# Splits of turned queries and outputs and the addition of normed sums, moved from VectorE to GpSimd

## The reference

```
cq = rms_norm(hidden_states @ w_qa.T, q_a_ln_w)
q = (cq @ w_qb.T).reshape(b, s, H, DQ).transpose(0, 2, 1, 3)
q_pe = q_pe * cos + rotate_half(q_pe) * sin
...
scores = jnp.einsum('bhqd,bhkd->bhqk', q_full, k_full) * scale
scores = jnp.where(causal, -jnp.inf, scores)
attn = jax.nn.softmax(scores.astype(jnp.float32), axis=-1)
out = jnp.einsum('bhqk,bhkd->bhqd', attn, v)
return out @ w_o.T
...
x = x + _layernorm(_L0_attn_ref(_layernorm(x, axis=-1), ...), axis=-1)
```

## Time and profile before

| | us |
|---|---|
| median of 3 runs | 1697.91 |
| lowest to highest | 1697.68 to 1703.39 |
| the profiled execution, its own time | 1701.13 |
| its span on the core | 1699.4 |
| VectorE busy, whole span | 1182.0 (70%) |
| ScalarE busy, whole span | 1020.6 (60%) |
| GpSimd busy, whole span | 306.5 (18%) |
| TensorE busy, matmul records | 1560.8 (92%) |

### The profile page before, as it was taken

The page is one execution under the profiler, slowest core; times in us unless marked ns, Lnnn a source line. Parts: engine busy times, 40 slices in busy tenths (PEclk is TensorE's granted clock), DMA queues, the critical chain, the costliest instruction groups (busy, mean ns, idle before and its releaser), DMA issues. The chain is left out here.

```text
span 1699.4 us, 38029 instructions
## 1 busy us (share of the span) xinstructions
PE 1560.8 (92%) x14452; PEld 1309.5 (77%) x14452; DVE 1182.0 (70%) x2472; ACT 1020.6 (60%) x2009; POOL 306.5 (18%) x752
## 2 busy tenths in 40 slices
PE   6789998999999999999999999999839999989997
PEld 4577787877788788888888888888727877867886
DVE  4567777776777777787787788778655546576564
ACT  3456665765666666677677667667524455545573
POOL 5411111111111211211211121221000002020231
PEclk9889999999999999999999999999969999999999
DMA  7000000000000000000000000000013100000000
GB/s 221 0 1 1 2 2 1 2 2 2 1 2 2 1 2 2 1 2 2 2 2 2 2 2 2 2 2 2 2 41 84 40 1 1 1 29 13 1 26 25
DMA packets 27524, 22.47 MB, mean 13 GB/s; under 512 B 9660, under 2 KB 25148, under 8 KB 27220
## 3 DMA queue, kind: packets, MB, share of 16 engines
q1 hardware_dynamic: 27348, 20.05, 4.1%
HBM read 17.95 MB, written 2.10 MB: 12 GB/s over the span
## 5 line engine op out<-in xcount | busy, mean ns | idle before, releaser
L784 ACT ACTIVATE pT_hi<-pT 128x512 f16<-128x512 f32 (+3 forms) x640 | 341.5, 534 | 302.7 <-PE pT L702 300.1
L905 DVE TENSOR_TENSOR pT_lo<-pT,pT_hi 128x512 f16<-128x512 f32 (+3 forms) x640 | 387.6, 607 | 147.5 <-ACT pT_hi L784 141.3
L773 ACT ACTIVATE pr<-pS,nmx 128x512 f32<-128x512 f32 (+3 forms) x640 | 401.1, 627 | 21.6 <-DVE nmx L896 19.8
L893 DVE TENSOR_REDUCE cmx<-pS 128x1 f32<-128x512 f32 x576 | 339.0, 617 | 65.4 <-PE pS L689 60.9
L702 PE MATMUL pT<-ident,pr 128*128 128x128 f32 x2176 | 348.3, 276 | 16.0 <-DVE pT_lo L905 14.5
L702 PEld LDWEIGHTS pT<-ident,pr 128*128 128x128 f32 x2176 | 253.1, 140 | 54.9 <-ACT pr L773 23.8
L687 PE MATMUL pS<-lT_hi,qT_hi 128*128 128x512 f32 (+2 forms) x640 | 281.5, 440 | 4.2 <-ACT pr L773 2.7
L744 PE MATMUL pO<-c_hi,pT_hi 128*128 128x65 f16 x2176 | 265.7, 194 | 18.4 <-DVE O L923 17.8
L745 PE MATMUL pO<-c_lo,pT_hi 128*128 128x65 f16 x2176 | 266.5, 193 | 0.0
L746 PE MATMUL pO<-c_hi,pT_lo 128*128 128x65 f16 x2176 | 263.7, 192 | 0.0
L1308 PE MATMUL pGU<-lT_hi,W_all 128*128 128x512 f32 (+1 forms) x640 | 221.1, 405 | 16.1 <-ACT sgb L1388 12.1
(11 more groups left out here) (268 smaller groups left out, 2461.5 us busy)
## 6 DMA issues: line engine op xcount, KB each, us to landing
X<-in_x SPq DMA_DIRECT2D x4, 512.0 KB, 6.2
wo<-in_w_o SPq DMA_DIRECT2D x1, 2048.0 KB, 11.1
out<-X SPq DMA_DIRECT2D x8, 256.0 KB, 2.0
raw<-in_wd SPq DMA_DIRECT2D x14, 128.0 KB, 2.2
raw<-in_wg SPq DMA_DIRECT2D x13, 128.0 KB, 2.7
raw<-in_wu SPq DMA_DIRECT2D x13, 128.0 KB, 2.6
wqn<-in_w_qn SPq DMA_DIRECT2D x1, 1536.0 KB, 16.3
raw<-in_qg SPq DMA_DIRECT2D x6, 128.0 KB, 2.5
```

The source lines that it names most:

```text
L773: act.activation(pr[:, at % RING, 0:n * P], pS[at % 4][:, 0:n * P], ACT.Exp, bias=nmx[:, p % 4:p % 4 + 1]).then_inc(sem("exped"), 1)
L784: act.activation(pT_hi[:, a % 4, 0:chunk[a][2] * P], src, ACT.Copy).then_inc(sem("t_hi"), 1)
L893: ch.inc(dve.tensor_reduce(cmx[:, p % 2, c:c + 1], pS[at % 4][:, 0:n * P], AX.X, ALU.max))
L905: dve.tensor_tensor(pT_lo[:, a % 4, 0:w], src, pT_hi[:, a % 4, 0:w], ALU.subtract).then_inc(sem("t_lo"), 1)
```

## The change

New f32 tiles in SBUF, two buffers each, take the turned queries (`q32`) and the turned outputs (`o32`). ScalarE copies PSUM to them; it no longer writes `qT_hi` and `OT_hi`. GpSimd makes both halves from the copy: a copy (hi) and a subtraction (lo). The bank pQ is free after ScalarE's copy, and so is pT after o_turn (`lo_until` counts VectorE's subtractions without those of o_turn). `sum` waits for the new semaphore `o_split`. `y_add` moves to GpSimd, at its place in the plan, and `x_measure` on VectorE waits for it by `x_added`, as it did when both were VectorE's.

```diff
+                q32 = sbr(loop, "q32", [P, 2, HG * P])
+                o32 = sbr(loop, "o32", [P, 2, 4, P])
...
+                lo_until = [sum(k[0] != "o_turn" for k in t_items[:n]) for n in range(len(t_items) + 1)]
...
                             elif what == "turn":
-                                pe.wait_ge(sem("q_hi"), i + 1)
-                                pe.wait_ge(sem("q_lo"), i + 1)
+                                pe.wait_ge(sem("q_out"), i + 1)
...
                                 pe.wait_ge(sem("t_hi"), n - 1)
-                                pe.wait_ge(sem("t_lo"), n - 1)
+                                pe.wait_ge(sem("t_lo"), lo_until[n - 1])
...
-                            done = t_index["o_turn", (u, 1)] + 1
-                            pe.wait_ge(sem("t_hi"), done)
-                            pe.wait_ge(sem("t_lo"), done)
+                            pe.wait_ge(sem("o_split"), o_index["o_turn", (u, 1)] + 1)
...
-                        def q_hi(i):
+                        def q_turned_out(i):
                             act.wait_ge(sem("q_turned"), i + 1)
-                            act.activation(qT_hi[:, i % 2], pQ[:], ACT.Copy).then_inc(sem("q_hi"), 1)
+                            if i >= 2:
+                                act.wait_ge(sem("q_lo"), i - 1)
+                            act.activation(q32[:, i % 2], pQ[:], ACT.Copy).then_inc(sem("q_out"), 1)
...
-                                u, k = a
-                                if u >= 2:
-                                    act.wait_ge(sem("y_summed"), u - 1)
-                                act.activation(OT_hi[:, u % 2, 4 * k:4 * k + 4], src.rearrange("p (j n) -> p j n", j=4),
-                                               ACT.Copy).then_inc(sem("t_hi"), 1)
+                                m = o_index[step]
+                                if m >= 2:
+                                    act.wait_ge(sem("o_split"), m - 1)
+                                act.activation(o32[:, m % 2], src.rearrange("p (j n) -> p j n", j=4), ACT.Copy).then_inc(sem("t_hi"), 1)
...
+                        def split_q(i):
+                            pool.wait_ge(sem("q_out"), i + 1)
+                            pool.tensor_copy(qT_hi[:, i % 2], q32[:, i % 2]).then_inc(sem("q_hi"), 1)
+                            pool.wait_ge(sem("q_hi"), i + 1)
+                            pool.tensor_tensor(qT_lo[:, i % 2], q32[:, i % 2], f(qT_hi[:, i % 2]), ALU.subtract).then_inc(sem("q_lo"), 1)
+
+                        def split_o(a):
+                            u, k = a
+                            m = o_index["o_turn", a]
+                            ks = slice(4 * k, 4 * k + 4)
+                            pool.wait_ge(sem("t_hi"), t_index["o_turn", a] + 1)
+                            if u >= 2:
+                                pool.wait_ge(sem("y_summed"), u - 1)
+                            ch.inc(pool.tensor_copy(OT_hi[:, u % 2, ks], o32[:, m % 2]))
+                            ch.wait()
+                            pool.tensor_tensor(OT_lo[:, u % 2, ks], o32[:, m % 2], f(OT_hi[:, u % 2, ks]), ALU.subtract).then_inc(sem("o_split"), 1)
+
+                        def y_add(u):
+                            t = tiles_in_order[u]
+                            pool.wait_ge(sem("y_deviation"), u + 1)
+                            if u:
+                                pool.wait_ge(sem("x_added"), u)
+                            pool.tensor_scalar(tmp[:, u % 2], yb[:, u % 2], rs[:, t:t + 1], nmr[:, t:t + 1], ALU.mult,
+                                               ALU.add).then_inc(sem("y_read"), 1)
+                            pool.wait_ge(sem("y_read"), u + 1)
+                            pool.tensor_tensor(X[:, t, :], X[:, t, :], tmp[:, u % 2], ALU.add).then_inc(sem("x_added"), 1)
...
+                            elif step == "turn":
+                                split_q(at)
+                            elif step == "o_turn":
+                                split_o(at)
+                            elif step == "y_add":
+                                y_add(at)
```

More of the change, by code:

```diff
@@ L116, in build @@
                      "states_turned", "lambda_out", "exp_lambda", "w_float", "alpha", "one_less", "beta", "eps_ready",
-                     "g_up", "u_up", "w_up", "k_roped", "c_split", "kln_in", "wv_in", "wo_in", "wk_in", "wqn_in", "wqp_hi", "unit_made", "unit_hi", "unit_lo", "q_normed", "sums_out", "deviated", "x_normed", "t_turned", "t_hi", "t_lo", "y_copied", "y_stats", "y_deviation", "x_stats", "x_deviation", "xn_made",
+                     "g_up", "u_up", "w_up", "k_roped", "c_split", "kln_in", "wv_in", "wo_in", "wk_in", "wqn_in", "wqp_hi", "unit_made", "unit_hi", "unit_lo", "q_normed", "q_out", "o_split", "sums_out", "deviated", "x_normed", "t_turned", "t_hi", "t_lo", "y_copied", "y_stats", "y_deviation", "x_stats", "x_deviation", "xn_made",
                      "dma_x0", "dma_x1", "dma_x2", "dma_x3", "w_in0", "w_in1", "w_in2", "w_in4"):
@@ L631, in build @@
                 t_index = {s: n for n, s in enumerate(t_items)}
+                o_index = {s: n for n, s in enumerate(k for k in t_items if k[0] == "o_turn")}
+                lo_until = [sum(k[0] != "o_turn" for k in t_items[:n]) for n in range(len(t_items) + 1)]
                 widths = {"probs": lambda at: chunk[at][2] * P, "o_turn": lambda a: 4 * P, "x_turn": lambda a: KD * P}
@@ L735, in values @@
                             pe.wait_ge(sem("t_hi"), done)
-                            pe.wait_ge(sem("t_lo"), done)
+                            pe.wait_ge(sem("t_lo"), lo_until[done])
                             if c == 0 and p % HG == 0 and p:
@@ L819, in _ @@
                             elif step == "turn":
-                                q_hi(at)
+                                q_turned_out(at)
                             elif step in ("probs", "o_turn", "x_turn"):
@@ L876, in _ @@
                         ch = Chain(dve, sem("dve_step"))
-                        def q_lo(i):
-                            dve.wait_ge(sem("q_hi"), i + 1)
-                            dve.tensor_tensor(qT_lo[:, i % 2], pQ[:], f(qT_hi[:, i % 2]), ALU.subtract).then_inc(sem("q_lo"), 1)
                         def maximum(at):
@@ L905, in t_lo @@
                                 dve.tensor_tensor(pT_lo[:, a % 4, 0:w], src, pT_hi[:, a % 4, 0:w], ALU.subtract).then_inc(sem("t_lo"), 1)
[L906 to L910, removed]
                             else:
@@ L931, in y_measure @@
                             dve.bn_aggr(mv[:, t, :], stats[:, t, :]).then_inc(sem("y_stats"), 1)
[L933 to L939, removed]
                         def x_measure(u):
@@ L946, in x_measure @@
                             dve.bn_aggr(mv[:, t, :], stats[:, t, :]).then_inc(sem("x_stats"), 1)
-                        own_steps = {"y_measure": y_measure, "y_add": y_add, "x_measure": x_measure}
+                        own_steps = {"y_measure": y_measure, "x_measure": x_measure}
                         turned = None
@@ L955, in _ @@
                                 maximum(at)
-                            elif step == "turn":
-                                q_lo(at)
-                            elif step in ("probs", "o_turn", "x_turn"):
+                            elif step in ("probs", "x_turn"):
                                 turned = (step, at)
```

## The result

The changed kernel took 1704.35 us (median of 20 runs, 1701.76 to 1708.17); the kernel before, on the same chips, 1699.8 (20 runs, 1696.81 to 1703.41). (The ratio is not the quotient of the medians; one kernel's times scatter by some 6 us, so the two can differ by a microsecond.) The profiled execution took 1708.17 us for a span of 1706.4, the slowest of its 20, 7.0 above the profiled one of before (1701.13, span 1699.4).

What follows compares the result with a forecast made beforehand. TensorE was taken to set the loop's pace; start and tail +4.3, late additions +6 and gains -8 gave +2.3 us: 1703.4 us for the profiled execution, 1700.2 for the median, with a range of 1688 to 1711.

Steps and rivals of the forecast that it cites:

- GpSimd's prices: At 512 columns, 1.27 us for a two-input operation and 0.61 for the copy; the addition's scaling 0.55, its sum 0.73.
- The cover of the splits: In the loop's body, later splits cost nothing; the tightest cover, at light tiles, is 2.7 us, 1.4 after the change.
- The start: At the loop's start, the first scores wait for the first queries' split with nothing beside it: +1.3 us.
- The tail: At the loop's end, last split 1.3, last addition queued behind a deviation 1.2 and slower by 0.5: +3.0 us.
- The late additions: At four odd tiles from the 8th on, the addition queues behind GpSimd's rope and VectorE waits: 4 x 1.5 = +6 us.
- The gains: In the loop, earlier free banks, early even additions off VectorE, and shorter waits for pT_lo and O: -8 us together.
- Three sums' bank: At three sums, the queries' bank is free with ScalarE's copy instead of VectorE's subtraction: 0.7 us each, 2.1 won.
- the even early additions: At three even early tiles, about 0.45 of the addition's 0.87 us off VectorE arrives: 1.3 us won.
- VectorE's relief: In the loop's body, shorter waits for pT_lo 3.0 and O 1.0, plus 0.5 for the turned outputs' bank.
- The relief: Rival: half of TensorE's waits for pT_lo and O goes throughout the loop, -12 us, 1686 us; chance 0.12.
- The wrong queue: Rival: VectorE's wait for x_added spreads to all eight odd tiles, +13 us, 1711 us; chance 0.12.
- The shared port: Rival: VectorE's remaining operations stretch by 0.2 us wherever GpSimd is busy, +19 us, 1719 us; chance 0.04.

Runs made afterwards that it cites:

- The slowed splits: Three more copies of 512 columns before the subtraction of each queries' split, against the kernel with the addition early: 1703.17 us.
- the kernel with the addition early: The changed kernel with GpSimd's addition right behind its deviation, in front of the rope and the next tile's deviation: 1693.87 us, 0.9963 of before.

## Why the prediction was right, and where it was not

**GpSimd's prices** held: 1.28 us for a two-input operation of 512 columns (1.27 worked out from the earlier trace rows), 0.61 for the copy (its lower bound, as taken), 0.56 and 0.73 to 0.74 for the addition.

**The cover of the splits** held; TensorE waits for qT_lo once, at the start, and 2.80 us is the 2.8 named. The slowed splits show that the tightest cover is what the earlier trace rows gave.

**The start**, +1.3: measured 1.3 (2.80 - 1.51).

**The tail**, 3.0: measured 4.6 (6.1 - 1.5). Split 1.3 and addition 1.7 to 1.9 are as priced; missing from the sum are the 1.5 us of the last sum at the lower clock. A wait of 2.8 in front of it instead of 1.5 was costed as 1.3 and no more. (The clock does not always fall here: the kernel with the addition early has the same split in the tail and does its last sum at 1.00.)

**The late additions**, +6: the waits are at the four places named, 1.4, 1.4, 1.2 and 0.8, 4.8 together, and VectorE's idle time there is 1.5 to 2.1 us. The step "there is no slack, so the 1.6 goes through" was right and too short: 3.7 us of clock went with it in the profiled execution. This is the term that was mis-sized, 8.5 for 6.

**The gains**, 8: measured 8.4 (9.4 less 1.0 of clock at the start). Three sums' bank gave 0.7, 0.75 and 0.75, 2.2 for 2.1; the even early additions 0.4, 0.5 and 0.5 for 1.3 together; VectorE's relief of the queries' subtraction 2.5 to 3.7 and of the outputs' 0.9, for 3.0 + 1.0 + 0.5. One gain was not in the sum: the additions of the 9th, 11th and 13th tile too, off VectorE, bring 0.5 to 0.7 each (1.7 in the kernel with the addition alone). Together with the splits the additions bring 2.0 (8.4, and 6.4 with the splits alone), not the 2.8 that they bring by themselves, so the parts overlap; the total came out near the count in part for that reason.

Without the clock the terms come to 1.3 + 4.8 + 3.1 - 8.4 = +0.8, where +2.3 was forecast; with 1.0 that the phase before the loop was late and 3.7 + 1.5 - 1.0 of clock, +6.0 at the loop's end (measured 6.1). The 0.9 us up to 7.0 lie behind the loop, in code that the change doesn't touch: some 0.5 are made up by 1285 us, and 1.5 go near 1561 us, where the clock is at 0.50 for 3.4 us and was at 1.00 at this place in before. By the medians the kernel was 4.6 slower, 2.3 more than forecast; a typical run so has less of the clock's loss than the profiled one: twelve of the 20 runs took 1701.8 to 1705.8 us at a mean clock of 0.973 to 0.976, the other eight, the profiled one among them, 1706.6 to 1708.2 at 0.972. So the range held, but the forecast was low by a cost that it did not have at all, and the waits, overestimated by 1.2, made up for part of it; that the median came so near is in part luck, and the profiled execution lies 4.8 above the 1703.4 forecast for it. Another 1.9 us of the 4.2 between 1700.2 and 1704.35 is the base: the median of three runs of before was 1697.9, that of twenty 1699.8.

**The rivals.** The relief did not spread: O's wait went from 17.8 to 17.1 only. The wrong queue was the right mechanism in four places, not eight; the early odd tiles had 0.2 to 1.2 us to spare (0.4 to 1.2 in the prediction), and what is late there costs nothing. The shared port did nothing in the changed kernel; pT_lo's mean is 609 ns over its four forms (607 before). The kernels with the load put back show both cases: a subtraction of two SBUF operands beside GpSimd's cast stretches it to 1.13 us, a reduction of one operand leaves it at 0.61. The Trainium skill (SBUF — State Buffer, Who interferes with whom) says that a VectorE instruction with two SBUF inputs contends with a GpSimd instruction that reads SBUF, and one with at most one SBUF input, outside the two-port modes, does not; the traces agree, 1.13 and 0.61 us. The Trainium skill's sentence (Perfetto Trace Analysis, Optimizing Scalar/DVE Operations) that moving operations between the two "might not help" is not borne out here: most of what moved, VectorE had read from PSUM, and in the right order the move is worth 6.7 us by the medians.

## What to carry to other kernels

When work moves to an engine with a queue of its own, place it in that queue anew: the changed order of one addition was worth 11.3 us, more than the move itself. Price a new wait of the engine that sets the pace not by its length alone, but with an extra term for the clock: of four new waits that cost 0.8 to 1.4 us by themselves one cost 2.5 us more by it, one 1.2, two nothing, and no reading of the trace of before told which. And at the two ends of a loop, where nothing lies beside the moved step, leave it on the faster engine: the first split, the last one and the last two additions were worth 5.5 us (6.7 and 12.2 below before), 3.7 of them inside the loop.

## What the runs showed of the hardware

TensorE's granted clock fell from 1.00 to 0.50 (2.4 to 1.2 GHz) in the middle of the loop, behind new waits. It stayed there for 6.8 us where TensorE had worked 0.39 us in 3.5, and for 3.4 us where it had worked 1.43; behind 0.87 in 3.5 it stayed at 1.00 in the changed kernel and fell in one with two additions moved. In code behind the loop that all kernels share, a stretch of 3.4 us at 0.50 is in eleven profiles and missing in three, and costs 1.5 us. Four transposes took 1.05 us instead of 0.60 at the lower clock. GpSimd's cast of 512 columns took 1.13 instead of 0.61 us beside a VectorE subtraction of two SBUF tiles, and VectorE's own up to 1.42 for 0.69.
